# Moving a far branch ahead of the expert layer, loading and turning the first rows by halves behind filler matmuls, and taking the last sums by halves

## The reference, cut to what matters

```python
x = x + _L0_xattn_ref(_layernorm(x, axis=-1), ctx_1024, ctx_1024)    # gelu(x @ ctx.T) @ ctx, per batch, 1601 context rows
x = x + _L0_ffn_ref(_layernorm(x, axis=-1), Wg, W1, W2)             # 8 experts, top-k of tokens per expert, gelu(xt @ W1[e]) @ W2[e]
x = x + _L1_xattn_ref(ctx_1024, _layernorm(x, axis=-1), mask, ...)  # 16 heads, masked softmax over context rows, @ Wo.T
x = x + _L1_ffn_ref(_layernorm(x, axis=-1), ...)                    # one of 8 experts per batch, chosen by its last row
```

## Time and profile before

| What | Value |
|---|---|
| median of three executions | 701.31 us |
| profiled execution: its time / its span | 702.61 us / 700.80 us |
| TensorE busy | 646.9 us, 92% of the span |
| VectorE busy | 331.7 us, 47% |
| ScalarE busy | 253.9 us, 36% |
| GpSimd busy | 72.9 us, 10% |
| chain that ended last: TensorE / VectorE / issue / DMA | 73% / 16% / 4% / 3% |
| granted TensorE clock, mean | 0.993 of full speed |

### The profile page before, as it was taken

How to read it: one execution, slowest core, us unless ns; L and a number is a source line. 1 busy time by engine, 2 the same in 40 slices (tenths; PEclk the granted TensorE clock), 3 DMA queues, 4 the chain that set the end, 5 groups by cost and what they waited for, 6 DMA issues and landing times.

```text
span 700.8 us, 8971 instructions
## 1 busy us (share of the span) xinstructions
PE 646.9 (92%) x3149; PEld 363.7 (52%) x3156; DVE 331.7 (47%) x981; ACT 253.9 (36%) x369; POOL 72.9 (10%) x75
## 2 busy tenths in 40 slices
PE   3999999999998888999997899999999998899997
PEld 1666666666666555666664533334334334255443
DVE  4334233103005673222644978677987986412100
ACT  0111111111112332332232456654755764753321
POOL 0000000000002002444412000000030030012000
PEclk9999999999999999999999999999999999999999
DMA  8992401503000212341325512031331002200500
GB/s 311 358 366 91 144 0 61 196 0 112 16 1 30 74 57 93 142 130 60 121 62 147 145 32 83 3 102 42 84 93 53 2 2 62 61 1 0 179 32 30
DMA packets 47889, 62.73 MB, mean 90 GB/s; under 512 B 8768, under 2 KB 40738, under 8 KB 47330
## 3 DMA queue, kind: packets, MB, share of 16 engines
q1 hardware_dynamic: 45122, 55.65, 24.8%
q0 software_dynamic: 2720, 6.50, 3.0%
HBM read 44.03 MB, written 11.49 MB: 79 GB/s over the span
## 4 chain that ended last, share of the span: by engine, by line
PE 73%; DVE 16%; issue 4%; DMA 3%; ACT 2%; POOL 0%; SPq 0%; DVEq 0%; POOLq 0%; ACTq 0%
PE ps L569 13%; PE ps L580 13%; DVE arena L1997 6%; PE ps L1023 6%; PE ps L1082 4%; PE ps L791 4%; PE ps L761 4%; PE ps L872 4%; PE ps L1067 4%; PE ps L880 3%; PE ps L842 2%; PE ps L733 2%; PE ps L828 2%; PE ps L890 2%; PE ps L1085 1%
## 5 line engine op out<-in xcount | busy, mean ns | idle before, releaser
L1997 DVE TENSOR_REDUCE arena<-ps 128x1 f32<-128x416 f32 x256 | 145.1, 585 | 30.5 <-PE ps L1023 27.6
L1406 ACT ACTIVATE arena<-ps 128x1024 f32<-128x1024 f32 (+1 forms) x112 | 104.8, 964 | 67.2 <-PE ps L1067 49.5
L569 PE MATMUL ps<-xnT,arena 128*128 128x512 f32 x208 | 101.9, 615 | 0.9 <-DVE xnT L1525 0.9
L580 PE MATMUL ps<-arena 128*128 128x256 f32 x416 | 99.8, 384 | 0.0
L580 PEld LDWEIGHTS ps<-arena 128*128 128x128 f32 x416 | 80.7, 194 | 33.7 <-issue 25.0
L1215 ACT ACTIVATE arena<-ps 128x512 f32<-128x512 f32 x52 | 31.0, 597 | 175.9 <-PE ps L569 175.9
L1023 PE MATMUL ps<-arena 97*128 97x416 bf16 x256 | 82.0, 345 | 11.2 <-issue 4.7
L1023 PEld LDWEIGHTS ps<-arena 97*128 97x128 bf16 x256 | 23.7, 96 | 92.7 <-DVE arena L1997 35.8
L1067 PE MATMUL ps<-arena 100*128 100x512 bf16 x192 | 56.8, 379 | 2.2 <-DMA arena<-arena 1.5
L1525 DVE COPY xnT<-ps 128x512 f32<-128x512 f32 x16 | 10.4, 686 | 100.8 <-PE ps L542 100.8
L569 PEld LDWEIGHTS ps<-xnT,arena 128*128 128x128 f32 x208 | 39.9, 195 | 30.7 <-issue 28.5
(11 more groups left out here) (232 smaller groups left out, 731.3 us busy)
## 6 DMA issues: line engine op xcount, KB each, us to landing
arena<-in_W SPq DMA_DIRECT2D x16, 512.0 KB, 10.0
arena<-in_ctxT SPq DMA_DIRECT2D x4, 1664.0 KB, 7.7
arena<-in_ctxN SPq DMA_DIRECT2D x4, 1664.0 KB, 12.8
arena<-arena SPq DMA_DIRECT2D x48, 128.0 KB, 2.7
arena<-last_k_parts SPq DMA_DIRECT2D x48, 104.0 KB
last_k_parts<-arena SPq DMA_DIRECT2D x24, 104.0 KB, 1.8
x_tok<-in_x SPq DMA_DIRECT2D x4, 512.0 KB, 9.3
xn_rows<-xn SPq DMA_DIRECT2D x4, 512.0 KB, 5.6
```

The costliest lines, as they stand in the source:

```text
L569: ins = pe.matmul(ps[:, 4 + k % 2, :], ctxT_s[:, b % 2, c, f * P:f * P + P], xnT[:, c, S * b:S * b + S], start=(c == 0), stop=(c == KC - 1))
L580: ins = pe.matmul(ps[:, b % 2 * 2 + t // 2, t % 2 * D:t % 2 * D + D], hid[:, (k - 2) % 4, t * P:t * P + P], ctxN_s[:, b % 2, f, :], start= ...
L1406: act.activation(pexp2[:, u % 4, 0:n, :], ps[:, 2 + 2 * (u % 2):2 + 2 * (u % 2) + n, :], ACT.Exp).then_inc(f_pe, 1)
L1997: dve.tensor_reduce(cmax2[:, h, j:j + 1], ps[:, banks.place(key), 0:KF], AX.X, ALU.max).then_inc(banks.is_taken(key), 1)
```

## The change

It has three parts.

**1. The start.** The load of batch 0's rows is split into two DMAs of two tiles. VectorE takes the statistics per half, and a new semaphore tells when two of the four tiles are normed. TensorE begins with 26 filler matmuls of 128x512 bf16 on a tile of ones, which VectorE now writes itself by a memset, and then turns the tiles by halves. The first hidden product waits for each column half by itself.

**2. The last sums of the first layer.** The sums of the last two context blocks are issued tile by tile, so that the first two tiles end ahead of the others. VectorE adds and takes statistics by halves, norms by halves, and TensorE turns by halves. The logits go through one column half first (`last_logits`). `keep_busy(6)` is `keep_busy(2)`.

**3. The branch.** The router's tail and the expert stage become a function `experts()` on each engine, called first in `general_way()` and in `fast_way()`. The branch now stands ahead of it. `keep_busy(4)` is gone; TensorE reads `near` before the last batch is turned.

```diff
+            def transposes_by_halves(b, n):
+                banks = [tp_bank() for k in range(KC)]
+                for half in range(2):
+                    if half == 0:
+                        pe.wait_ge(s_half, n)
+                    else:
+                        pe.wait_ge(s_ln, 1 if n == 1 else 2 * B)
+                    for k in range(KC):
+                        for t in range(TB // 2 * half, TB // 2 * half + TB // 2):
+                            ins = pe.transpose(banks[k][:, t * P:t * P + P], xn[:, TB * b + t, k * P:k * P + P], eye)
+                        if half == 1:
+                            ins.then_inc(s_tpr, 1)
+
+            pe.wait_ge(s_zt, 2)
+            for _ in range(26):
+                pe.matmul(ps[:, 0, :], ones_b[:, :], ones_b[:, :].unsqueeze(1).broadcast_to([P, TB, P]), start=True, stop=True, skip_group_check=True)
             pe.wait_ge(s_const, 16)
-            pe.wait_ge(s_ln, 1)
-            transposes(xn, 0)
+            transposes_by_halves(0, 1)
...
+            def last_logits(b):
+                o = tp_bank()
+                for k in range(KC):
+                    if k == KC - 1:
+                        pe.wait_ge(s_tpf, tp[0] - 1)
+                    for t in range(TB):
+                        ins = pe.matmul(o[:, t * E:t * E + E], xnT[:, k, S * b + t * P:S * b + t * P + P], wg[:, k, :],
+                                        start=(k == 0 and t == 0), stop=(k == KC - 1), skip_group_check=True)
+                ins.then_inc(s_tpr, 1)
...
-                        pe.wait_ge(s_tpf, KC * (b + 1) if b < 3 else KC * 4 + MASK_TURNS)
+                        if b > 0:
+                            pe.wait_ge(s_tpf, KC * (b + 1) if b < 3 else KC * 4 + MASK_TURNS)
...
                     for c in range(KC):
+                        if k == 0:
+                            pe.wait_ge(s_tpf, c + 1)
...
+                    if k < NK:
+                        use_hidden(k - 2, range(TB)).then_inc(s_mm2, 1)
+                    elif k == NK + 1:
+                        for t in range(TB):
+                            use_hidden(k - 3, (t,))
+                            ins = use_hidden(k - 2, (t,))
+                            if t % 2 == 1:
+                                ins.then_inc(s_mm2, 1)
...
+            pe.wait_ge(s_list, 1)
+            near = pe.value_load(lst_i[0:1, 33:34], min_val=0, max_val=NC - 1)
             pe.wait_ge(s_res, 4)
-            keep_busy(6)
-            for b in range(3, 4):
-                pe.wait_ge(s_ln, 5 + b)
-                transposes(xn, b)
-                logits(b)
+            keep_busy(2)
+            transposes_by_halves(B - 1, 2)
+            last_logits(B - 1)
...
-            keep_busy(4)
-            pe.wait_ge(s_exp8, 3)
...
             def fast_way():
+                experts()
                 banks = fast_banks
...
-            dve.wait_ge(s_x[0], 16)
-            layer_norm(0)
+            dve.memset(ones_b[:, :], 1.0).then_inc(s_zt, 1)
+            for half, s_part in enumerate((s_x[0], s_gat2)):
+                dve.wait_ge(s_part, 16)
+                for t in range(TB // 2 * half, TB // 2 * half + TB // 2):
+                    ins = dve.bn_stats(stats[:, t, :], x_tok[:, t, :])
+            ch.step(dve, ins)
+            aggregates(0)
+            norm_by_halves(0)
...
+            last = B - 1
+            ch.step(dve, add_last_rows(0, 2, NF * B - 1))
+            for t in range(2):
+                dve.bn_stats(stats[:, TB * last + t, :], x_tok[:, TB * last + t, :])
+            add_last_rows(2, 4, NF * B).then_inc(s_res, 1)
+            dve.wait_ge(s_res, B)
+            for t in range(2, 4):
+                ins = dve.bn_stats(stats[:, TB * last + t, :], x_tok[:, TB * last + t, :])
+            ch.step(dve, ins)
+            aggregates(last)
+            norm_by_halves(last)
+            take_columns(last)
+            take_logits(last)
...
-            sp.dma_start(x_tok[:, 0:TB, :], a["x"][0:S, :].rearrange("(t p) d -> p t d", p=P)).then_inc(s_x[0], 16)
+            for lo, s_part in ((0, s_x[0]), (TB // 2, s_gat2)):
+                sp.dma_start(x_tok[:, lo:lo + TB // 2, :], a["x"][lo * P:(lo + TB // 2) * P, :].rearrange("(t p) d -> p t d", p=P)).then_inc(s_part, 16)
```

More of the change, by code:

```diff
@@ L558, in logits, with use_hidden @@
                 ins.then_inc(s_tpr, 1)
+            def last_logits(b):
[7 more added lines that the diff above has]
+                ins.then_inc(s_tpr, 1)
+            def use_hidden(k, tiles):
+                b, f = divmod(k, NF)
+                for t in tiles:
+                    ins = pe.matmul(ps[:, b % 2 * 2 + t // 2, t % 2 * D:t % 2 * D + D], hid[:, k % 4, t * P:t * P + P], ctxN_s[:, b % 2, f, :],
+                                    start=(f == 0 and t % 2 == 0), stop=(f == NF - 1), skip_group_check=True)
+                return ins
             for k in range(NK + 2):
@@ L799, in expert_pair, with experts @@
                         query_rest(0, 1, 1, QUERY_BANKS[0][1])
[L801 to L805, removed]
+            def experts():
+                pe.wait_ge(s_exp8, 3)
+                for t in range(NT):
+                    if t == NT // 2:
+                        keep_busy(1)
+                    if t % (NT // 2) == 0:
+                        pe.wait_ge(s_oh, t // (NT // 2) + 1)
+                    ins = pe.matmul(ps[:, 1, 0:2 * IDX], pos_b[:, t, :], tok_b[:, t, :, :].rearrange("p a b -> p (a b)"),
+                                    start=(t == 0), stop=(t == NT - 1), skip_group_check=True)
+                ins.then_inc(s_ohp, 1)
+                pe.wait_ge(s_ekp, KC * B)
+                pe.wait_ge(s_ev, 2 * B)
+                keep_busy(11)
+                pe.wait_ge(s_slot, 1)
+                first_pairs = pe.value_load(be_i[0:1, NBLK:NBLK + 1], min_val=1, max_val=PAIRS - LAST_PAIRS)
+                pe.wait_ge(s_w12, 16 * 2 * E)
+                pe.wait_ge(s_xsb, 32)
+                block_transposes()
+                with pe.Fori(0, first_pairs) as i:
+                    expert_pair(i, -1)
+                for s in range(LAST_PAIRS):
+                    expert_pair(first_pairs + s, s)
+                pe.wait_ge(s_expd, 1)
             def turn_queries(b):
@@ L1603, in _ @@
             active_chunks()
-            for b in range(B):
+            for b in range(B - 1):
                 dve.wait_ge(s_mm2, NF * (b + 1))
```

192 lines of the change are left out of this document (96 added, 96 removed).

## The result

The changed kernel takes 695.1 us (693.94 to 695.83) against 701.09 us before, each the median of six executions: ratio 0.991, 95% interval 0.989 to 0.992. The medians are 6.0 us apart. The profiled execution took 695.33 us with a span of 693.5. The two spans differ by 7.3 us, since the profiled execution of before lay 1.5 us above the median of its runs and this one 0.2 us.

The account below looks back on a forecast made before the run. It took TensorE to carry most of the chain of waits. The terms 4.3 + 1.1 + 4.2 + 1.2 - 2.0 = 8.8 us, off the median 701.31, gave 692.5 us, with a range of 687 to 699.5.

Parts of the forecast that it names:

- the larger chance: Whole kernel: faster by more than 1%, below 694.3 us, given chance 0.60.
- the router's jump: TensorE's far jump at the router's end, begun 1 us ahead of the last record: list 1.2 to 2.5 late, -2.0 us.
- the full 1.35: Roots of the last sums: upper end of the gain, 1.35 us earlier; 0.2 was taken.
- The start: 4.3: Part 1: earlier first product (2.1) and full clock (2.5) less 0.3 save 4.3 us; ends 1.0 and 5.0.
- A wait of the first product for `ctxT`: Sign at the start: the first hidden product waiting for this load would make the prediction wrong; landing forecast at 10.2.
- term (c): Start, clock: twelve product records take 5.2 instead of 7.72 us, 2.5 saved, less 0.3 for fillers ending late.
- The last sums: 1.1: Part 2: roots 0.2 and turning plus logits 0.9 save 1.1 us; ends -1.0 and 2.3.
- The rival "hidden": Router's end: the jump is hidden behind queued matmuls, giving 690.5 us; chance 0.12.
- The stall behind the experts: After the experts: 4.28 us of issue goes, less 0.1 for a remaining ScalarE wait, saving 4.2 us.
- the half clock behind it: Behind the experts' stall: half-rate fillers, transposes and products go too, saving 1.2 us, between 0.4 and 2.5.
- Fillers too late: Rival at the start: fillers do not raise the clock in time, 1.0 instead of 4.3, 695.8 us; chance 0.11.
- The loop's jump back: Rival in the expert loop: each of six turns fetches again, 16 to 26 us, 709 to 718 us; chance 0.06.

Follow-up runs that it names:

- e1: The kernel before with part 1 alone (two loads, 26 fillers, turning by halves): 697.01 us, ratio 0.994.
- e9: The changed kernel with its 26 fillers at the start cut from 512 to 8 columns: 697.27 us, ratio 0.994 against before.
- e6: The changed kernel with GpSimd's clears of the value buffers waiting for the last norm as well: 690.62 us, ratio 0.985 against before.
- e2: The kernel before with part 2 alone (last sums, norm, turn and logits by halves, two fillers instead of six): 702.89 us, ratio 1.002.
- e3: The kernel before with part 3 alone (branch ahead of the experts, four fillers gone): 698.07 us, ratio 0.996.
- e10: The kernel before with part 2 alone and GpSimd's clears moved behind the last norm: 699.37 us, ratio 0.997.
- e11: The changed kernel with GpSimd's clears behind the last norm and keep_busy(4) ahead of the branch: 689.26 us, ratio 0.982 against before.
- e5: The changed kernel with keep_busy(6) instead of keep_busy(2) ahead of the last batch's turning: 692.27 us, ratio 0.986 against before.
- e4: The changed kernel without its 26 fillers at the start: 699.24 us, ratio 0.996 against before.
- e8: The changed kernel with keep_busy(2) between the first token transposes and the first expert pair: 692.85 us, ratio 0.988 against before.
- e7: The changed kernel with keep_busy(4) back ahead of the branch: 694.72 us, ratio 0.990 against before.

## Why the prediction came close, and where it failed

The sum was 8.8 us; the spans differ by 7.3, the medians by 6.0, so 695.1 came where 692.5 was forecast. The sign and the range held; the larger chance (faster by over 1%) did not. In the spans, part 2 came 1.9 us short of its term and the first pair took 1.6 that no term had, while the router's jump cost 1.2 less than its term and small rows gave 0.8 more: that the sum is off by only 1.5 is in part luck. (The lower end of the range, 687, is what all upper ends give with the full 1.35; without it, as the text says, they give 688.5.)

- **The start: 4.3, measured 4.30 in the spans and 4.1 in e1.** Right, in part by errors that cancel. The first product started 1.99 us earlier (2.1 forecast), and from there to the first sums it took 2.3 less (2.2 forecast). Inside the first of these, the first normed tile began at 7.84, not 9.05, 1.2 earlier where the text gave 0.4, so its column half was out at 10.65, not 11.25; and `ctxT` was there at 11.40, where the text had 10.2. A wait of the first product for `ctxT` was named as a sign that the prediction is wrong. It came, 0.75 us behind the copy, and took back only what the earlier norm had brought. Nor are the fillers worth the 2.2 of term (c): turning by halves makes TensorE start earlier, and in e9, with hardly any filler work, the twelve records took 6.85 us and not 7.72, so that the halves bring 3.1 and the fillers 1.2, within the 1 us said above.
- **The last sums: 1.1, measured -0.82. This step failed.** "Four fillers fewer leave TensorE idle for some 2 us where it had 0.9" was right to 0.1 us, and the price that the text put only into its lower end came true: the sixteen records took 1.63 us longer, and the logits part lost 1.04 where the text chose +0.65. The nearest row was the slow start of the earlier trace rows, half rate behind an idle stretch, and I weighed the gain of the earlier copy above it. The turning gained 0.22 (0.3 forecast). The roots gained 0, not 0.2: they were held to the end of the clears, as the 1.94 us ending within 0.02 us of them show, and the 0.17 without them (e6). By the Trainium skill, "SBUF — State Buffer", Who interferes with whom, whoever of the two issues first has the pair of SBUF ports that VectorE and GpSimd share for the whole instruction. The trace agrees that VectorE waits, but here it was held through two clears: the second began at 212.89, and VectorE had its turn only behind that one. In e2 it was held for one:

```profile
214.33 1.68 DVE L1536 TENSOR_SCALAR var_eps<-mv 128x4 f32<-128x4 f32 x1
...
215.92 0.34 POOL L2426 MEMSET arena<- 128x128 f32 x1
...
216.04 0.24 DVE L1537 TENSOR_SCALAR rstd<-var_eps 128x4 int32<-128x4 int32 x1
```

There it came free at 216.01, between the long clear (over at 215.99) and the end of the short one, and its successor took 0.24 instead of 0.17 and ended with the short clear. So both things that the text foresaw happen, holding through or slipping between.

- **The first expert pair: not foreseen, 1.56 us lost.** The granted clock over it, before and then in the changed kernel:

```profile
274.70:278.40 3.70, 3.70 (x10) 1.74 (x11) 0.00 (x0) 0.60 (x1) 0.95 (x1) 1.00 0.23 71
```

```profile
271.90:277.00 5.10, 5.05 (x8) 2.22 (x9) 0.00 (x0) 0.60 (x1) 0.95 (x1) 0.68 0.46 167
```

Before's pair ran wholly at 2.4 GHz; this one spent about 3.3 us at 1.2 GHz, and the matmuls are the same. The idle ahead of it is alike (1.33 here, 1.32 in e3 and e6 with a fast pair). All thirteen kernels, in us:

| Kernels | 16 logit records | second one-hot set | 22 fillers behind it | first pair |
|---|---|---|---|---|
| before, e1, e10, e11 | 1.95 to 2.31 | 0.37 to 0.38 | 5.0 | 3.7 |
| e3, e5, e6 | 1.95 | 0.57 to 0.58 | 5.6 to 6.5 | 3.7 |
| e4, e8 | 3.45, 3.57 | 0.58 | 6.99, 7.08 | 3.7 |
| changed, e2, e9 | 3.58 | 0.37 to 0.38 | 5.0 | 5.26, 5.39, 5.39 |
| e7 | 3.58 | 0.37 | 5.0 | 3.69 |

The pair was fast wherever the logits were fast, and it was fast in all five kernels where the clock had fallen at the jump (e3, e4, e5, e6, e8). There it had come back during the fillers, at a price that the pair does not show: in e8 1.2 of the 1.6 us that a fast pair brings were lost between the logits and the pair. Of the four kernels with slow logits and no fall at the jump, three had a slow pair, and e7, with four fillers ahead of the branch, did not. So slow logits alone don't settle it, e7 has one profile, and **its cause stays open.** The size is surer: between e2 and e10 the root step differs by 1.5 us, the logits by 1.5 and the pair by 1.7, 4.7 together, and what they save by 4.3.
- **The router's jump: -2.0, measured -0.77.** The text had it begin 1 us ahead of the last product's end and cost 4.28, so TensorE was to be back 3.24 us behind that product, at full or at half clock (1.2 or 2.5 us late). It was back after 2.87 us and at full clock. Other kernels came out otherwise: without fillers there the idle was 2.56 to 3.36 us, and in e3, e4, e5, e6 and e8 the clock was down behind it. e3, 1.5 us late, lies inside the forecast. The rival "hidden" was nearer to the changed kernel than my figure, though the jump is not hidden: e7 shows the part that queued matmuls cover.
- **The stall behind the experts: 4.2, measured 4.23; the half clock behind it 1.2, measured 1.40.** Both right.
- **The rivals.** Fillers too late: they ended at 9.27, and no product ran slowly. The loop's jump back: none of the twelve kernels has a stall per turn; the largest idle by "issue" inside the loop is one of 0.2 to 0.4 us in most of them, and before has it too (0.40). The kind of danger was real, though: e4 shows a stall of 3.03 us that is gone in e9, where as many instructions stand ahead as in the changed kernel. That it depends on where the code lies is argued from this pair, not measured. It is in line with the fetch by pages of the Trainium skill, "Runtime: NRT & Kernel Launch", Instruction fetch mechanics; no run here shows the page's border itself.

Part by part and in medians the account closes: e1, e2 and e3 add up to 5.3 of 6.0.

## What to carry over

An engine sped up can run into a lock or an idle that its old lateness had mostly avoided: ask what else starts at the same moment (here GpSimd's clears), and what the other engine does while it waits. Count fillers by the idle that they leave, not by their number: four fewer cost 1.6 us at the logits, more than the earlier sums were to bring (1.35). A far branch is cheapest where its engine has nothing to do anyway, and an edit that changes the count of instructions can add or remove a stall elsewhere, so look for "issue" behind the branch before blaming the edit.

## What the runs showed of the hardware

- A far jump on TensorE shows as 3.96 to 4.28 us of "issue" at the loops' end, where every engine waits (before, e1, e2, e10), and as 2.56 to 3.36 us of idle behind the last value product (the changed kernel, e3 to e6, e8, e9). Part of the second may lie beneath the product itself, as e7 suggests; why it is shorter was not tried.
- The same jump was followed by a second stall of 3.03 us two matmuls on in e4's profile, and not in e9's, whose only difference is 26 matmuls of 8 columns, and the wait ahead of them, some 250 us earlier.
- The sixteen thin matmuls (8 columns, f32) took 3.45 to 3.58 us in all six kernels where 1.9 to 2.1 us of idle stood ahead of the turning (the changed kernel, e2, e4, e7, e8, e9), and 1.95 to 2.31 in the seven where 0.3 to 0.9 did (before, e1, e3, e5, e6, e10, e11). In five of these seven the granted clock fell over the last of them or within a few us behind them all the same (not in before and e5).
- A VectorE `tensor_scalar` of 128x4, 0.17 us alone, took 0.68, 1.68 and 1.94 us beside GpSimd's clears (before, e2, the changed kernel), ending with a clear each time within 0.02 us.
